# Fewer semaphore waits in the tile loop of a mixture-of-experts block, ten places for z, and TensorE without its filler products

## The reference

```python
# cross-attention; the inputs are layer-normed x and the context
x = x + softmax(q @ k.T / sqrt(D)) @ v @ Wo.T + bo
# mixture of experts on xt = layernorm(x), 8 experts, top 2 by router probability
h = layernorm(relu(xt @ W1[e] + b1[e]), g1[e], be1[e])     # 128 -> 512
y = layernorm(relu(h @ W2[e] + b2[e]), g2[e], be2[e])      # 512 -> 128
x = x + sum over the token's two experts of gate * y
```

## Time and profile before

| | us |
|---|---|
| median of 3 runs (lowest, highest) | 324.51 (323.78, 324.84) |
| the profiled execution | 324.29 |
| its span, first to last instruction | 322.7 |
| routing stage, about | 0 to 145 |
| tile stage, about | 145 to 303 |
| answers back and output | 303 to 322.7 |
| mean granted clock of TensorE | 0.903 of full |

### The profile page before, as it was taken

How to read it: one execution, slowest core, us unless ns; L and a number is a source line. 1 busy time by engine, 2 the same in 40 slices (tenths; PEclk the granted TensorE clock), 3 DMA queues, 4 the chain that set the end, 5 groups by cost and what they waited for, 6 DMA issues and landing times.

```text
span 322.7 us, 10282 instructions
## 1 busy us (share of the span) xinstructions
PE 254.7 (79%) x2960; PEld 201.9 (63%) x2960; DVE 232.2 (72%) x1091; ACT 211.9 (66%) x795; POOL 190.3 (59%) x300
## 2 busy tenths in 40 slices
PE   3997547899385738758977889998889888899995
PEld 3455445556273715237866787997789787788631
DVE  1789648343476385667876778898799888889975
ACT  2467445628282739716776788797799788789830
POOL 9403728562717073738566766686668666677660
PEclk9999859579859596859999999999999999999999
DMA  6994941211311311435231222332223555541337
GB/s 182 351 286 138 289 162 44 69 56 43 122 37 58 106 51 59 98 70 129 64 76 52 61 60 66 66 62 63 62 63 87 148 141 134 117 117 29 101 123 242
DMA packets 48675, 34.56 MB, mean 107 GB/s; under 512 B 26870, under 2 KB 42742, under 8 KB 48619
## 3 DMA queue, kind: packets, MB, share of 16 engines
q1 hardware_dynamic: 38972, 22.80, 25.7%
q0 software_dynamic: 6592, 9.00, 9.8%
q10 hardware_dynamic: 3056, 2.11, 2.1%
HBM read 15.11 MB, written 12.02 MB: 84 GB/s over the span
## 4 chain that ended last, share of the span: by engine, by line
PE 31%; ACT 18%; another core or an unknown queue 17%; issue 17%; DVE 13%; DVEq 1%; DMA 1%; ACTq 1%
PE bank L721 19%; PE bank L725 11%; ACT rh L1353 2%; DVE kq L1894 2%; ACT cxT L1376 2%; ACT ex L1181 2%; ACT vv L1365 2%; DVE vo L1901 2%; ACT xt L1204 1%; ACT rg L1388 1%; ACT square_mask L1360 1%; DMA wr<-in_L_ffn_Wr 1%; DVE cx L1931 1%; ACT xT L1128 1%
## 5 line engine op out<-in xcount | busy, mean ns | idle before, releaser
L667 POOL DMA_INDIRECT slot_rows<-pay,pos x64 | 65.1, 1017 | 61.3 <-DVE pay L1765 44.3
L679 POOL DMA_INDIRECT answers<-vo,words_of x71 | 70.7, 995 | 43.0 <-ACT vo L1395 29.9
L1353 ACT ACTIVATE rh<-bank 128x512 f16<-128x512 f32 x71 | 41.5, 585 | 26.2 <-remote 21.7
L721 PE MATMUL bank<-kb_room,w1h 128*128 128x128 f16 x568 | 56.3, 220 | 0.8 <-issue 0.7
L725 PE MATMUL bank<-w2h,rh 128*128 x284 | 51.6, 219 | 3.1 <-ACT rh L1353 2.5
L725 PE MATMUL bank<-rh 128*128 128x129 f16 x284 | 51.7, 220 | 1.0 <-issue 0.9
L721 PE MATMUL bank<-kb_room,w1l 128*128 128x128 f16 x284 | 51.6, 220 | 0.4 <-issue 0.3
L725 PE MATMUL bank<-w2l,rh 128*128 x284 | 51.5, 219 | 0.5 <-issue 0.5
L725 PE MATMUL bank<-w2h,kq 128*128 x284 | 40.5, 222 | 11.2 <-DVE kq L1894 8.0
L1894 DVE SCALAR_TENSOR_TENSOR kq<-bank,rh 128x512 f16<-128x512 f32 x71 | 47.9, 675 | 0.5 <-ACT rh L1353 0.4
L1901 DVE CUSTOM_DVE_ANT_0 vo<-bank,square_mask 128x257 f32<-128x257 f32 x71 | 29.9, 421 | 23.8 <-ACT square_mask L1360 22.1
(11 more groups left out here) (259 smaller groups left out, 635.7 us busy)
## 6 DMA issues: line engine op xcount, KB each, us to landing
x_tok<-in_x SPq DMA_DIRECT2D x8, 256.0 KB, 7.1
w1f<-in_L_ffn_W SPq DMA_DIRECT2D x2, 1024.0 KB, 9.3
pay<-pay SPq DMA_DIRECT2D x8, 256.0 KB
w1f<-answers SPq DMA_DIRECT2D x8, 256.0 KB
w2f<-answers SPq DMA_DIRECT2D x8, 256.0 KB, 2.9
kb_room<-slot_rows SPq DMA_TRANSPOSE x71
words_of<-slot_rows POOLq DMA_DIRECT2D x71, 1.0 KB
answers<-vo,words_of POOLq DMA_INDIRECT x71
```

What stands on the lines that cost most here:

```text
L667: eng.indirect_dma_start(slot_words, bass.IndirectOffsetOnAxis(ap=pos[:, g % 2, k, i:i + 1], axis=0), pay[g % 2][:, k, i, :].bitcast(U32), ...
L679: eng.indirect_dma_start(answers, bass.IndirectOffsetOnAxis(ap=words_of[:, j % NW, 0:1], axis=0), z[j % NZ], None).then_inc(s_ans[j % NZ], 16)
L721: return eng.matmul(dst, lhsT, rhs, start=start, stop=stop)
L1353: eng.activation(rh_all(j), psH[j % 3][:, :].rearrange("p (c n) -> p c n", c=FC), ACT.Relu).then_inc(s_rh, 1)
```

## The change

Three edits. Guard waits that follow from other waits of the program are left out on ScalarE and VectorE. z gets ten places, five of them in the context tile `cx`, which is free by then, and `words_of` has ten instead of twelve; since `words` of tile j waits for the answer of tile j - 10, the wait in `scaled` goes, and the last five tiles wait in `answer` on GpSimd. `keep` and its calls go.

```diff
-        NW, NS, LEAD = 12, 8, 2
+        NW, NS, LEAD = 2 * NZ, 8, 2
...
-        z = [vo_all[:, n * D:(n + 1) * D] for n in range(3, 3 + NZ)]
+        z = [vo_all[:, n * D:(n + 1) * D] for n in range(3, 3 + NZ)] + [cx[:, n, :] for n in range(3, 3 + NW - NZ)]
...
             def answer(j):
                 eng.wait_ge(s_z, j + 1)
+                if j + NZ >= SLOT_TILES:
+                    eng.wait_ge(s_ans[j % NZ], answered(j - NZ))
...
-                    z[j % NZ], None).then_inc(s_ans[j % NZ], 16)
+                    z[j % NW], None).then_inc(s_ans[j % NZ], 16)
...
-            def keep(n):
-
-                for _ in range(n):
-                    mm(bank[2][:, 3 * P:], ones_b, ones_b)
...
                 if n == 1:
-                    keep(12)
                     ranks(0)
...
                 if n < GROUPS:
-                    keep(10)
                     probT(n)
...
-                    keep(10)
                     ranks(n - 1)
...
             def relu1(j):
                 eng.wait_ge(p_h, j + 1)
-                if j >= 3:
-                    eng.wait_ge(p_y, j - 2)
...
             def sum_(j):
                 eng.wait_ge(p_y, j + 1)
-                if j >= 2:
-                    eng.wait_ge(s_s2, j - 1)
...
             def std1(j):
-                if j >= 4:
-                    eng.wait_ge(s_rs, rooted(j - 2))
...
             def relu2(j):
-                if j >= 3:
-                    eng.wait_ge(s_w, j - 2)
...
             def std2(j):
-                if j >= 2:
-                    eng.wait_ge(s_rs, rooted(j))
...
             def scaled(j):
                 eng.wait_ge(s_rg, j + 1)
-                if j >= NZ:
-                    eng.wait_ge(s_ans[j % NZ], answered(j - NZ))
-                eng.activation(z[j % NZ], w_[j % 3], ACT.Copy, scale=rg[j % 4][:, :]).then_inc(s_z, 1)
+                eng.activation(z[j % NW], w_[j % 3], ACT.Copy, scale=rg[j % 4][:, :]).then_inc(s_z, 1)
```

More of the change, by code:

```diff
@@ L725, in mm_beside @@
                 return eng.matmul(dst, lhsT, rhs, start=start, stop=False, skip_group_check=True)
-            ones_b = ones[:, :].bitcast(BF16)[:, 0:P]
-            def keep(n):
-                for _ in range(n):
-                    mm(bank[2][:, 3 * P:], ones_b, ones_b)
             done = []
@@ L1891, in r_lo @@
                 eng.wait_ge(s_rh, j + 1)
-                if j >= 2:
-                    eng.wait_ge(p_y, j - 1)
                 eng.scalar_tensor_tensor(out=rl[j % 2][:, :, :], in0=psH[j % 3][:, :].rearrange("p (c n) -> p c n", c=FC),
@@ L1898, in square_sums @@
                 eng.wait_ge(s_hsum, j + 1)
-                if j >= 4:
-                    eng.wait_ge(s_vv, j - 3)
                 eng.tensor_tensor_reduce(squares[:, :], psY[j % 3][:, D:D + 2 * P + 1], square_mask[j % 2][:, :], 1.0, 0.0,
@@ L1911, in affine @@
                 eng.wait_ge(s_rs, rooted(j + LAG1))
-                if j >= 3:
-                    eng.wait_ge(s_ur, j - 2)
                 eng.scalar_tensor_tensor(out=u[j % 3], in0=psY[j % 3][:, 0:D], scalar=rs1(j),
@@ L1922, in aggr2 @@
                 eng.wait_ge(s_st2, j + 1)
-                if j >= 4:
-                    eng.wait_ge(s_std2, j - 3)
                 eng.bn_aggr(mv2[j % 4][:, :], st2[j % 4][:, :]).then_inc(s_ag2, 1)
@@ L1928, in gained @@
                 eng.wait_ge(s_ag2, j + 1)
-                if j >= 3:
+                if j + LAG2 - 1 >= SLOT_TILES:
                     eng.wait_ge(s_z, j - 2)
@@ L1937, in roots @@
                     eng.wait_ge(s_std1, p - LAG1 + 1)
-                if p >= LAG2:
+                else:
                     eng.wait_ge(s_std2, p - LAG2 + 1)
-                if p >= LAG2 + 4:
-                    eng.wait_ge(s_z, p - LAG2 - 3)
                 eng.reciprocal(rs[p % 4][:, :], sd[p % 4][:, :]).then_inc(s_rs, 1)
```

## The result

| | before | after |
|---|---|---|
| median us (lowest, highest), 4 runs each | 324.14 (322.89, 324.84) | 314.02 (310.63, 363.31) |
| the profiled execution, us | 324.29 | 310.63 |
| its span | 322.7 | 309.0 |
| mean granted clock of TensorE | 0.903 | 0.884 |

The ratio is 0.9618, 95% interval 0.9543 to 0.9693: faster. It rests on the changed kernel's two fast executions, 310.63 and 312.62 us; those of 315.42 us (mean granted clock 0.873) and 363.31 us (0.622) are left out of it, though not out of the median.

What follows compares the result with a forecast made beforehand. No engine was full over the whole span; the prediction blamed late TensorE counts in routing, and VectorE and TensorE for a tile's cost. From 324.29 us, -4.6 - 4.6 - 3.1 + 2 = -10.3 gave 314; range 300 to 327.

Steps and rivals of the forecast that it cites:

- Group 7's late count: Routing stage, copy `pT` after the transposes: TensorE's count, some 4.8 us late, would come in time, gaining 4.6 us.
- group 8's: Routing stage, VectorE's wait for the `mask` products: a count more than 4.5 us late would come in time, gaining 4.6 us.
- a rival: More late counts go, in the other routing groups too: 15 us more, 299 us; part may be given back; chance 0.14.
- Its reason for them: Routing stage, groups 7 and 8: ten dense small products during GpSimd's scatter separate late counts from those in time.
- The products on the chain: Routing stage, groups 4 to 7: ten unread products stand on the chain four times; removing them gains 3.1 us.
- The clock: Routing stage: without the products some full-clock stretches fall to half, losing 2 us, bounds 0 and 8.
- The waits: Tile stage, ScalarE and VectorE: removing satisfied guard waits gains 0, as they lie under instructions that run anyway.
- The bound of 2 us: Tile stage: the most that removing VectorE's satisfied waits could gain if their cover were partly gone.
- z and `words`: Tile stage: moving the waits for answers costs 0; bound one more idle piece, +1.7 us.
- The tile stage unchanged: From 145 to 303 us: steady step of 1.86 us kept, idle time before `relu1` again 17 to 26 us.
- a shift of three pieces: Tile stage: three more or fewer late counts before `relu1`, 4.7 us either way, in every case.
- the signs named in advance: Profile after: waits in groups 7 and 8 under 1 us, longer half-clock routing stretches, tile step and `relu1` idle time unchanged.

Runs made afterwards that it cites:

- the series: Follow-up kernels with each tile's turning transfer replaced by a plain one; the kernel before so treated took 267.98 us, ratio 0.9992 to itself unaltered on that chip.

## Why the prediction came out

The time was right: 314.0 predicted, 314.02 measured, inside 300 to 327. That the two agree to 0.02 us is luck: the median lies between executions of 310.63 and 315.42 us, and by the ratio the gain is 12.4 us, not 10.1. The sum behind it was right only in part. By its steps:

- **Group 7's late count, -4.6, and group 8's, -4.6.** Both went, as forecast: 5.20 to 0.50 us and 4.96 to 0.70. But the late pieces of the routing stage fell by 6.7 us in all (36.5 to 29.8), not by 9.2, because others took their place, group 4's 9.29 above all, of which the kernel before had 1.3. And in time group 8's brought 0.3 us, not 4.6. The prediction named this danger (an earlier release moves work into another scatter) under a rival and didn't put it in the sum.
- **Its reason for them is not shown, and partly falls.** It took the ten products of ones during the scatter to be what makes a count late. In the kernel after, counts are late without any such product (7.4 us in group 4), and on the chip of the series they come in time with the products and the scatter in place. The products are neither needed nor enough. Nor are the late counts TensorE's alone: VectorE's wait of 1.36 us in group 7 is for its own. What makes counts late stays open; that they moved when TensorE's stream lost 142 products and the other queues their waits is all that is seen, in one profile of each kernel.
- **The products on the chain, -3.1.** It fits: -2.9 by the two lines of span against clock, which are fits and no direct measurement.
- **The clock, +2.** Right in sign, undersized: 3.7 to 5.0 us on the chip of the series by the same lines. In the first pair of profiles the routing stage's clock fell from 0.79 to 0.75, which has no price of its own there. In "TensorE: Matmul & The Clock Gate", "Why this matters for your kernels", the Trainium skill asks to keep TensorE fed so that it holds the full clock. The series, where no count is late, agrees: without the products the clock was 0.026 lower and the kernel 1% slower. In the first comparison the clock fell too, 0.903 to 0.884, and the kernel was 3.8% faster all the same.
- **The routing stage in sum.** -6.7 of late pieces and -5.1 measured leave 1.6 us lost by everything else, products and clock among it; the prediction had 1.1 gained by these two. Its 10.3 us were to come from this stage alone, which gave half.
- **The waits, 0.** Right where it could be tested, on the chip without late counts: ratio 1.0002 with them out. The bound of 2 us was enough. The reason, VectorE full with the waits in place, holds too, and two more at each place show where it ends: +5 us.
- **z and `words`, 0.** Right: the 4.8 us of waits for an answer are gone in the changed kernel and in the waits-only one, none came in their place, and the ratio is that same 1.0002.
- **Slips that carry nothing.** 228 products in 13 us at 32 a tile give a step of 1.82 us, not 1.86 (the traces have 1.85); VectorE loses seven waits a tile, not six; a quarter of 29 busy us is 7.3, not 8.
- **The tile stage unchanged.** This step failed. It lost 8.5 us, by fewer late counts before `relu1`: 21.7 us in 14 pieces became 10.0 in 6. The prediction had the mechanism (late counts at places that TensorE's stream sets) as a shift of three pieces, 4.7 us, either way, and gave it no sign; it was 8 pieces fewer (of the 11.7 us, 3.2 came back as waits before `relu1` with TensorE as the named releaser, 4.5 to 7.7). The bound was too small by almost half.

So two errors met: 10.3 us expected from the routing stage where 5.1 came, and nothing from the tile stage where 8.5 came. The profiled execution gained 13.7, the medians 10.1. Of the signs named in advance, the short waits before group 7's `pT` and group 8's count and the unchanged step of a tile were seen, and the half-clock stretches took more of the routing stage (0.79 to 0.75 in the mean); the "remote" idle time before `relu1` was to be 17 to 26 us again and was 10.0.

And the gain was seen only where counts are late. On the chip of the series the change's parts are +1.0% (products) and 0.0% (waits and z); if they add up, the change that gained 3.8% there costs 1% here. That sum is argued, not measured.

## What to carry to other kernels

Add up the waits without a releaser in a program of one core before reasoning about anything else: here they came to 58 us of 324, and the same kernel on another chip was 55 us shorter. Run it there before crediting an edit with a gain; an edit that shifts such stalls looks like one that saves work. Measure a gain by when both kernels pass the same instruction, not by which stalls went. Read in the code which count a wait is for before blaming an engine. Satisfied waits were free here at one to a place, under an engine that was full, and cost 2% at three; products that nobody reads are worth their slots only where they keep TensorE's clock up, which the granted clock over many runs shows and a single profile does not.

## What the runs showed of the hardware

- One kernel, 268 us on one chip, 332 on another, and 324 in the first comparison, with the same instructions. The mean granted clock was 0.903 in the profile of 324 us and 0.948 in that of 268 to 269; at 1.9 us for 0.01 that would be 9 of the 55 us, part of which may itself follow from TensorE's idling. The late counts read off the first profile, 58 us, would cover the difference without it.
- Where counts are late, one can stand behind work that needed 0.4 us and be 7.4 us late (`probT` in group 4 of the changed kernel). The late ones stood in other places in the two kernels' profiles. VectorE's own count came late to VectorE too: 6.0 us before `oh` in the kernel before, 0.2 on the chip of the series.
- Executions of one kernel on one chip had mean granted clocks from 0.925 to 0.961, and their spans followed at 1.9 us for 0.01. The changed kernel's execution at 0.622 took 52.7 us more than the one at 0.884, 2.0 us for 0.01.
